# Three wide PSUM tiles instead of two in the first cross attention, and value projections of four key tiles at once

## The reference

```
q = layernorm(x) @ Wq ; k = context @ Wk ; v = context @ Wv      # per batch: 256 queries, 4096 keys
attn = softmax(q k^T / 4, over the 4096 keys, masked) ; x = x + (attn @ v) @ Wo
```

## Time and profile before

| | |
|---|---|
| runs | 2180.97 us median of 3 (2179.33 to 2189.02) |
| profiled execution | span 2176.0 us from its first to its last instruction, 34820 instructions; no other time of it is given |
| busy over the span | TensorE (PE) 83%, VectorE (DVE) 56%, ScalarE (ACT) 47%, GpSimd (POOL) 35% |
| 0 to 875 us (first stage) | of 875 us PE busy 785.0, ACT 542.9, DVE 269.6, POOL 318.1; DMA share 0.56 |
| 145 to 875 us | of 730 us PE busy 685.6, ACT 501.5, DVE 216.8; granted clock 1.00 |
| exponentials | 512, mean 1026 ns, the first at 55.9 us, the last at 871.1 us |
| score matmuls | 2048, mean 276 ns |
| value copies (line 613) | 128, mean 420 ns |

### The profile page before, as it was taken

How to read it: one execution, slowest core, us unless ns; L and a number is a source line. 1 busy time by engine, 2 the same in 40 slices (tenths; PEclk the granted TensorE clock), 3 DMA queues, 4 the chain that set the end, 5 groups by cost and what they waited for, 6 DMA issues and landing times. The chain is left out here.

```text
span 2176.0 us, 34820 instructions
## 1 busy us (share of the span) xinstructions
PE 1799.2 (83%) x13676; PEld 1100.0 (51%) x13676; DVE 1227.9 (56%) x3043; ACT 1025.8 (47%) x1381; POOL 760.4 (35%) x669
## 2 busy tenths in 40 slices
PE   5969999999999999888877877878777849888885
PEld 2424554455445444556556623545454437666663
DVE  5142424232342310263688379899999995558676
ACT  1447656756775688111130155656546531213552
POOL 6343424433533240000030027777878750110000
PEclk8989999999999999999977855877778779999887
DMA  6647555655646371200010001223132242000000
GB/s 144 113 109 125 118 118 103 125 104 118 119 112 123 81 118 48 76 2 1 2 51 1 14 1 45 80 59 88 46 87 73 59 179 93 1 1 1 1 6 15
DMA packets 78046, 150.01 MB, mean 69 GB/s; under 512 B 15464, under 2 KB 63144, under 8 KB 71464
## 3 DMA queue, kind: packets, MB, share of 16 engines
q1 hardware_dynamic: 64304, 101.80, 16.7%
q0 software_dynamic: 12768, 42.59, 12.8%
q10 hardware_dynamic: 792, 3.17, 0.4%
HBM read 93.59 MB, written 2.62 MB: 44 GB/s over the span
## 5 line engine op out<-in xcount | busy, mean ns | idle before, releaser
L571 ACT ACTIVATE P<-R 128x1024 f32<-128x1024 f32 x512 | 506.9, 1026 | 216.4 <-PE R L112 180.4
L112 PE MATMUL R<-QS,KST 100*128 100x256 bf16 x2048 | 296.3, 276 | 60.4 <-ACT P L571 53.2
L112 PEld LDWEIGHTS R<-QS,KST 100*128 100x128 bf16 x2048 | 169.6, 98 | 224.6 <-ACT P L571 121.0
L1810 POOL TENSOR_TENSOR ACC<-ACC,PM 128x4096 f32<-128x4096 f32 x22 | 195.1, 8867 | 1.8
L200 POOL TENSOR_TENSOR LNrs<-LNve,pk_const 128x2 f32<-128x2 f32 x36 | 25.3, 703 | 453.7 <-DVE LNve L196 453.3
L112 PE MATMUL R<-OV,QT 32*128 32x512 f32 x512 | 181.0, 793 | 0.0
L789 POOL DMA_DIRECT2D KST<-OV x300 | 144.5, 490 | 71.9 <-PE R L112 55.3
L112 PE MATMUL R<-P,VP 128*32 128x256 f32 x2304 | 154.8, 385 | 0.5 <-ACT P L571 0.3
L601 DVE CAST OV<-RT 128x512 bf16<-128x512 f32 x64 | 27.1, 423 | 210.8 <-ACT RT L116 140.2
L733 POOL CAST OV<-RT 128x512 bf16<-128x512 f32 x64 | 42.6, 665 | 259.9 <-DVE RT L604 259.9
L1800 POOL TENSOR_TENSOR SM<-SM,NG 128x1 f32<-128x1 f32 x30 | 79.2, 2640 | 146.2 <-DVE PM L1729 146.2
(11 more groups left out here) (372 smaller groups left out, 3543.6 us busy)
## 6 DMA issues: line engine op xcount, KB each, us to landing
KST<-OV POOLq DMA_DIRECT2D x276, 128.0 KB, 10.9
CT<-in_ctxP SPq DMA_DIRECT2D x40, 768.0 KB, 4.4
CN<-in_ctxn SPq DMA_DIRECT2D x60, 384.0 KB, 3.4
CT<-in_ctxT SPq DMA_DIRECT2D x64, 192.0 KB, 2.6
KST<-OV SPq DMA_DIRECT2D x84, 128.0 KB, 10.3
KST<-in_ctxP ACTq DMA_DIRECT2D x4, 768.0 KB, 9.4
QS<-x_q POOLq DMA_DIRECT2D x24, 128.0 KB, 5.4
pk_a<-in_pk_a SPq DMA_DIRECT2D x1, 3014.0 KB, 10.4
```

What stands on the lines that cost most here:

```text
L112: return e.matmul(o, l, r, start=st, stop=sp, skip_group_check=True)
L571: e.activation(P[(32 * p + k0) % 3][:, :], ring.at(("s", p, k0))[:, :], ACT.Exp).then_inc(*EX.up((p, k0)))
L1810: e.tensor_tensor(acc[:, :], acc[:, :], pm, ALU.add).then_inc(*G.up(("sum", p, h)))
```

## The change

- `ring` becomes R0, R1 and R2, three double tiles; `side` becomes the two single-bank tiles B0 and B1. `acc` of group p is always B(p mod 2), so every `tail`, `q`, `bound` and `out` product of a group uses the one other tile.
- A `k` job takes one `ring` tile, its two products in the two banks. A `v` job now makes four key tiles into one `ring` tile (two in each bank), with two VectorE copies of 512 columns, and there are 8 `v` jobs of a batch instead of 16.
- The steps: `k` at kt 18, 22, 26, 30 (before 14, 20, 26, 30); `v` of the next batch at kt 6, 10, ..., 30 of group 3 and the last at kt 2 of group 0 (before each even kt from 6, and kt 0, 2, 4); in batch 0 two of them before the scores and six at kt 0, 2, ..., 10.
- The `max` job, whose branch isn't entered, puts the ring's place back.

```diff
-    def take(self, key, *until, hold=False):
+    def take(self, key, *until, hold=False, at=None):
-        i = next(k % n for k in range(self.i + 1, self.i + 1 + n) if not self.held[k % n])
+        i = at if at is not None else next(k % n for k in range(self.i + 1, self.i + 1 + n) if not self.held[k % n])
...
-            ring, side = Slots(R[0:2]), Slots([R[2][:, 0:512], R[2][:, 512:1024], B2[0], B2[1]])
+            ring, side = Slots(R), Slots(B2)
...
-            q_steps, k_steps = [0, 12, 18, 24, 30], [14, 20, 26, 30]
+            q_steps, k_steps, v_steps = [0, 12, 18, 24, 30], [18, 22, 26, 30], [6, 10, 14, 18, 22, 26, 30]
...
-                if g == 3 and more and kt >= 6 and kt % 2 == 0:
-                    jobs.append(("v", b + 1, *divmod(kt // 2 - 3, 4)))
-                if g == 0 and b > 0 and kt in (0, 2, 4):
-                    jobs.append(("v", b, 3, kt // 2 + 1))
+                if g == 3 and more and kt in v_steps:
+                    jobs.append(("v", b + 1, *divmod(v_steps.index(kt), 2)))
+                if g == 0 and b > 0 and kt == 2:
+                    jobs.append(("v", b, 3, 1))
                 if b + g == 0 and kt % 2 == 0 and kt < 12:
-                    jobs += [("v", 0, *divmod(kt + 4, 4)), ("v", 0, *divmod(kt + 5, 4))]
+                    jobs.append(("v", 0, *divmod(kt // 2 + 2, 2)))
...
+                        o, free = ring.take(("k", b, tl, ch), (KC, (b, tl, ch, 1)))
+                        ps = [o[:, 512 * i:512 * i + 512] for i in range(2)]
...
+                        o, free = ring.take(("v", b, ch, h), (VC, (b, 4 * ch + h + 2)))
...
+                        for j in range(2):
+                            for i in range(2):
+                                c = (2 * h + j + 4 * i) * 128
+                                mm(e, o[:, 512 * i + 256 * j:512 * i + 256 * j + 256], t[:, c:c + 128], w["WvA"][:, :], j == 0, False)
+                        for j in range(2):
+                            for i in range(2):
+                                rows, c = slice(64 * i, 64 * i + 64), 1024 + (2 * h + j) * 128
+                                ins = mm(e, o[:, 512 * i + 256 * j:512 * i + 256 * j + 256], t[rows, c:c + 128], w["WvB"][rows, :], False, j == 1)
+                        ins.then_inc(*VPS.up((b, ch, h)))
...
-                        for s, k in side.take(("acc", p), hold=True)[1]:
+                        for s, k in side.take(("acc", p), hold=True, at=p % 2)[1]:
...
+                        for i in range(2):
+                            k2 = 4 * ch + h + 2 * i
+                            e.tensor_copy(VP[:, 2 * k2:2 * k2 + 2, 0:272].rearrange("p k (h d) -> p k h d", d=17)[:, :, :, 0:16],
+                                          ring.at(("v", b, ch, h))[:, 512 * i:512 * i + 512].rearrange("p (k h d) -> p k h d", k=2, d=16)).then_inc(*VC.up((b, k2)))
```

More of the change, by code:

```diff
@@ L307, in begin @@
                 jobs += [("q", 0, 2), ("k", 0, 0, 2), ("q", 0, 3), ("k", 0, 0, 3), ("q", 0, 4), ("bound", 0, 0, 0), ("v", 0, 0, 0), ("bound", 0, 0, 1)]
-                jobs += [("v", 0, 0, 1), ("bound", 0, 0, 2), ("v", 0, 0, 2), ("max", 0, 0), ("half", 0, 0, 1), ("v", 0, 0, 3)]
+                jobs += [("v", 0, 0, 1), ("bound", 0, 0, 2), ("max", 0, 0), ("half", 0, 0, 1)]
                 return jobs
@@ L350, in job @@
                         t, ts = tokens(n), slice(tl * 128, tl * 128 + 128)
[L351 to L356, removed]
+                        o, free = ring.take(("k", b, tl, ch), (KC, (b, tl, ch, 1)))
+                        ps = [o[:, 512 * i:512 * i + 512] for i in range(2)]
+                        for s, k in free:
+                            e.wait_ge(*s.at(k))
                         if n == 0:
@@ L366, in job @@
                     elif kind == "v":
-                        ch, r = at
+                        ch, h = at
                         n = chunk(b, 1, ch)
[L369 to L376, removed]
+                        t = tokens(n)
+                        o, free = ring.take(("v", b, ch, h), (VC, (b, 4 * ch + h + 2)))
+                        for s, k in free:
+                            e.wait_ge(*s.at(k))
+                        if b == 0 and ch + h == 0:
                             e.wait_ge(*LW.at("x0"))
-                        if r == 0:
+                        if h == 0:
                             e.wait_ge(*loaded(n))
[L380 to L386, removed]
+                        for j in range(2):
[7 more added lines that the diff above has]
+                        ins.then_inc(*VPS.up((b, ch, h)))
                     elif kind == "q" and at[0] == 1:
@@ L432, in job @@
                         base, done = 33 * (4 * b + g), 34 * (4 * b + g)
+                        last = ring.i
                         taken = [ring.take(("max", b, g, j)) for j in range(2)]
@@ L470, in job @@
                             ring.release(("max", b, g, j), *free)
+                        ring.i = last
                 for j in begin():
@@ L510, in weighted @@
                     if g == 0:
-                        e.wait_ge(*VC.at((b, kt)))
+                        e.wait_ge(*VC.at((b, kt // 2)))
                     e.wait_ge(*EX.at((p, kt)))
@@ L548, in job @@
                                 e.wait_ge(*KG.at(m - 3))
-                            acopy(e, RT[m % 3][:, :], side.at(("k", b, tl, ch, i))[:, :]).then_inc(*KC.up((b, tl, ch, i)))
+                            acopy(e, RT[m % 3][:, :], ring.at(("k", b, tl, ch))[:, 512 * i:512 * i + 512]).then_inc(*KC.up((b, tl, ch, i)))
                     elif kind == "max" and b + at[0] == 0:
@@ L605, in job @@
                     elif kind == "v":
-                        ch, r = at
-                        if b + ch + r == 0:
+                        ch, h = at
+                        if b + ch + h == 0:
                             e.wait_ge(*GI.at("ones"))
                         if b > 0:
[L610 to L614, removed]
+                            e.wait_ge(*PV.at((4 * b - 1, 8 * ch + 2 * h + 5)))
+                        e.wait_ge(*VPS.at((b, ch, h)))
+                        for i in range(2):
+                            k2 = 4 * ch + h + 2 * i
+                            e.tensor_copy(VP[:, 2 * k2:2 * k2 + 2, 0:272].rearrange("p k (h d) -> p k h d", d=17)[:, :, :, 0:16],
+                                          ring.at(("v", b, ch, h))[:, 512 * i:512 * i + 512].rearrange("p (k h d) -> p k h d", k=2, d=16)).then_inc(*VC.up((b, k2)))
                     elif kind == "q" and at[0] == 0:
@@ L781, in k_slots @@
                 if 4 * b + g == 1:
-                    e.wait_ge(*VPS.at((0, 3, 3)))
+                    e.wait_ge(*VPS.at((0, 3, 1)))
                 if 4 * b + g >= 2:
@@ L823, in job @@
                         ctx_load(e, chunk(b, 2 * tl, ch) + 2)
-                    elif kind == "v" and at[0] > 0 and at[2] == 3:
+                    elif kind == "v" and at[0] > 0 and at[2] == 1:
                         e.wait_ge(*VPS.at(at))
```

## The result

The changed kernel takes 2122.98 us (median of 4 runs, 2119.87 to 2124.38); the kernel before took 2181.11 on the same chip (4 runs, 2179.33 to 2189.02). The ratio is 0.9724, 95% interval 0.9707 to 0.9742. The forecast was 2123. The profiled run has a span of 2120.4 us, against 2176.0 before: 55.6 us less. The last exponential of the first stage starts at 814.3 instead of 871.1, which is 56.8 won; the rest of the span takes 1.2 us more. All that is to be explained lies in the first stage.

The account below looks back on a forecast made before the run. TensorE was taken to bound the first stage, losing time to score matmuls waiting for ScalarE's exponential. 82 us gained less 24 lost gave 58: span 2176 to 2118, plus 5 to the median, 2123 (range 2102 to 2150).

Parts of the forecast that it names:

- Steady pair: Two scores without a job beside, after 145 us: a third score tile brings 2.39 to 1.98 us, 59 us won.
- Value job: One job of four key tiles takes 2.98 us instead of 3.40 for two old ones: 10 us won over 24 jobs.
- Group 0 of batch 0: Last value job 5.4 us earlier, moving the slot-transfer chain; later key jobs leave 2 us less behind the stall: 7.4 won.
- The `side` tile: Group 1, batches 0 to 2: transposes of `q` wait for `tail`'s tile, stalling 5.1 us, 3.9 new: 12 us lost.
- The clock: The three gaps of 5.1 us in group 1 drop TensorE to its lower level: 2 us each, 6 lost.
- `bound` before `q`: At kt 18 the query product waits for VectorE to read `bound`'s tile: 0.8 us, x 3 = 2 us lost.
- Slot transfers in group 2: ScalarE's copy of the second key job waits for them, and group 3 may wait too: 4 us lost for three batches.
- The 5 us from span to median: The median of the runs lies 5 us above the profiled span, so 2118 became the forecast 2123.
- the free `side` tile: Rival: the shared tile in group 1 causes no stall or throttling; 76 us won, 2105; chance 0.13.
- the P buffers: Rival: ScalarE and the three P buffers become the bound, a steady pair staying at 2.18; 29 us won, 2152; chance 0.14.
- the replaced wait: Rival: P buffers take over the ring wait, a pair staying at 2.39 us; 2181, no change; chance 0.05.
- the lower clock: Rival: three new stalls keep TensorE at its lower level for long; 200 us there gives 28 us slower, 2209; chance 0.04.

Follow-up runs that it names:

- values_alone: The kernel before with value jobs of four key tiles, writing two `side` tiles; ring and key jobs stay: 2172.06 us, ratio 0.9958.
- root_first: The changed kernel, but in group 1 GpSimd computes the norm's root before issuing the slot transfers: 2106.29 us, ratio 0.966 to the kernel before.
- after_p4: The changed kernel with a fourth P buffer: 2124.28 us, ratio 0.9728 to the kernel before.
- ring_alone: The changed kernel, but with value jobs of two key tiles at their old steps, in ring tiles: 2138.5 us, ratio 0.9799 to the kernel before.
- tail_first: The changed kernel with the norm's job at kt 3 instead of 0, behind `tail` and its reciprocal: 2121.87 us, ratio 0.9722 to the kernel before.
- late_keys: `root_first` with key jobs at kt 24, 26, 28, 30 in group 0 of batch 0: 2098.52 us, ratio 0.9627 to the kernel before.
- late_keys_q: `late_keys` with the query product at kt 20 instead of 18, its transfers at kt 26 instead of 24: 2097.11 us, ratio 0.9603 to the kernel before.
- before_p4: The kernel before with a fourth P buffer, room coming from two overlaps of SBUF buffers: 2155.73 us, ratio 0.9874.

## Why the prediction was right

The medians agree to less than 1 us, which is partly luck. Term by term:

- **Steady pair.** Forecast 2.39 to 1.98, 59 us over 144 waits. Measured 1.98, and the waits are gone. Groups 13 to 15, which have no key, value or query jobs, took 33.8, 32.8 and 31.3 us where I had said 32 to 33; together 16.0 us won. Right, but for one wait of 1.3 us in group 13 (at 744.0).
- **Value job.** Forecast 2.98; measured 2.99, in ring tiles and in `side` tiles. The Trainium skill (TensorEngine Tiling (Array Packing), Key Properties) says that changing the tiling mode drains the engine; the trace agrees, as one job with one change instead of two jobs with two saves 3.40 - 2.99 = 0.41. That its gain needs the ring's third tile I had not seen: `values_alone` shows it.
- **Group 0 of batch 0.** Forecast 7.4. The period is 4.97 (4.96), the last value job comes 4.8 us earlier (5.4), the transfers land 4.7 us earlier, and the group is 8.8 us shorter. TensorE resumes 5.6 us earlier: before, it resumed 1.6 us behind ScalarE's copy, when the exponential was done as well; now its score has a free tile 0.65 us behind it (both from the copy's start). From there to group 1's first exponential it takes 14.9 us instead of 18.6, 3.7 less where I had counted 2 for the later key jobs. About 1 of this is an estimate for the clock, which was back 4.1 us behind the resumption instead of 6.5, at 0.43 us for each; no run separates it from the steps. The group is 1.4 us better than forecast.
- **The `side` tile.** Forecast a stall of 5.1 us, three times, released by the reciprocal, 3.9 of it new: 12 us. Measured 5.1, 5.1, 5.1, released so; with the 3.6 that the old kernel waited there, 11.7 are new. Group 1 was 42.7, 42.5 and 42.6 us, some 1.5 above the 41 that I had given.
- **The clock.** Forecast 2 us each, 6 in all. Measured 6.8 us at 0.50 at each stall, 3.8 to 4.9 of them behind it. By `root_first` it costs 1.2 to 2.2 us each, 20.7 - 15.3 = 5.4 in all; an estimate from the 4.9 + 3.8 + 4.5 us behind the stalls, at the prediction's 0.43 for each us, gives 5.7. The Trainium skill (TensorE: Matmul & The Clock Gate, HAM oscillation) says that idle gaps throttle the engine and each return is paid; the three stalls agree, each at less than the 3 us by which I had applied it, while `root_first`, without them, stays at 1.00 from 125 to 722 us.
- **`bound` before `q`.** Forecast 0.8 x 3 = 2; the row says 1.7, 3 times. Right.
- **Slot transfers in group 2.** Forecast 4 us. The second and third key jobs of group 2 start 7.74, 8.45 and 6.94 us apart in batches 0 to 2, and 2.98 + 2 x 1.98 = 6.94 is what they take without a wait: 0.8 + 1.5 + 0 = 2.3. No first score of a group waits for a transfer.
- **Not foreseen**: 3.4 us of gaps that end with "issue", in the waits above (2.9, and one of 0.5), the wait of 1.3 us in group 13, and 1.2 us in the rest of the span.

The sum: with costs of 15.3 - 3.6 + 5.4 = 17.1 for stall and clock, 1.7, 2.3, 3.4 and 1.3, the stage's 56.8 us won mean a gross gain of 82.6, near the forecast's 82. The gross gain is here the remainder, not measured by itself, so what agrees is the whole. The small terms missed in both directions and nearly cancelled: 1.4 more in group 0 (and so about 1 less in what remains of the gross gain), 2.3 instead of 4 and 17.1 instead of 18, against 3.4 + 1.3 + 1.2 that I had not counted. The 5 us from span to median were too many: the profiled run took 2122.22, 1.8 above its span, and that hid the 2.4 us by which its span was longer than 2118.

Of the rivals, the free `side` tile is refuted by the three stalls, the P buffers by `after_p4`, and the replaced wait by the pair of 1.98. The rival with the P buffers also had a slip in its price: half of 65 is 32, which leaves 26 won and 2155, not 29 and 2152. From the first exponential of group 1 on, the lower clock stayed at three stretches of 6.8 us, far from the 135 us from which it would have decided.

## What to carry to other kernels

When an engine gets faster, follow the chains that do not get faster and see where it now meets them; here one such meeting (a reciprocal behind a norm behind a queue of transfers) cost over a quarter of what the change won (16.7 of 58 us), and moving one group of GpSimd's instructions gave it back. A wait that the profile puts down to one buffer may be a loop through two; count both links before pricing a cure. Shortening work that fills another wait is worth little until that wait is gone, so two edits can be worth more together than the sum of each alone (here by some 7 us, in groups 3).

## What the runs showed of the hardware

TensorE has gaps in every version but the kernel before whose end the profile puts down to "issue", that is, to no semaphore. Timeline of the change:

```profile
581.37 0.64 PE L112 MATMUL B<-P,VP 128*32 128x256 f32 x8
...
584.14 0.64 PE L112 MATMUL B<-P,VP 128*32 128x256 f32 x8 [2.13 <-issue]
```

and of `ring_alone`, the timeline, the stretch of the gap, and the DMA queues from 592.5 to 596.6 (packets, MB, share):

```profile
591.92 0.64 PE L112 MATMUL B<-P,VP 128*32 128x256 f32 x8
596.59 1.08 PE L112 MATMUL B<-P,VP 128*32 128x256 f32 x8 [4.04 <-issue]
```

```profile
592.60:596.60 4.00, 0.01 (x1) 0.00 (x2) 0.00 (x0) 1.06 (x2) 0.00 (x0) 0.99 1.01 158
```

```profile
q0 software_dynamic: 121, 0.50, 77.5%
q1 hardware_dynamic: 29, 0.12, 17.8%
q8 instruction: 1, 0.02, 2.6%
```

The matmul stops in the middle of a run of 16, the DMA share is 1.01, and one packet of the instruction queue falls into the gap. In the change the same queue has a packet at the gap shown and at the wait that ends at 744.0, which the profile puts down to an exponential. It has none in the gaps of 0.8 and 0.5 us, and the 88 packets of the instruction queues in this stage leave one gap of 2 us; the kernel before has 89 and no gap. So a packet alone doesn't make one. The reading is that TensorE waits for its own next instructions behind the slot transfers; it fits, but no run took the traffic away from such a place, so it is not shown. In the stage such gaps sum to 3.4 us in the change, 4.1 in `root_first`, 5.6 in `tail_first`, 5.4 in `late_keys` and 8.8 in `late_keys_q`, to 1.9 in `values_alone` and 4.2 in `before_p4`, which still have two ring tiles, and to none in the kernel before. Behind the gap of `ring_alone` the granted clock was 0.50 for 3.4 us (596.5 to 599.9). The two fastest versions spread over 16 and 17 us between runs, the change over 4.5; whether these gaps are the reason stays open.
